# A graph network on one core: ring slots of eight gathered tiles with one store each, and landed slots counted one by one for SyncE

## The reference

```
def spline_conv(x, row, col, basis, idx, W, b):
    z = jnp.einsum('ni,kio->nko', x, W).reshape(N * K, Fout)        # K = 125
    gathered = z[col[:, None] * K + idx]
    msg = jnp.einsum('es,eso->eo', basis, gathered)
    out = jax.ops.segment_sum(msg, row, num_segments=N)
    deg = jax.ops.segment_sum(jnp.ones_like(msg[:, 0]), row, num_segments=N)
    return out / jnp.maximum(deg, 1.0)[:, None] + b

h = elu(spline_conv(ones, row, col, basis, idx, stn1_w, stn1_b))
h = elu(spline_conv(h, row, col, basis, idx, stn2_w, stn2_b))       # phase c2 below
t = elu(h @ stn3_w + stn3_b) @ stn4_w + stn4_b
new_pseudo = clip(pseudo + t[col] - t[row], 0, 1)
x = x + spline_conv(x0, row, col, basis2, idx2, conv_w, conv_b)     # phase c3 below
x = x + gat_and_gru(layer_norm(x), src, dst, ...)
```

## Time and profile before

| | us |
|---|---|
| median of 3 runs | 15551.18 (15526.23 to 15558.94) |
| the profiled execution's own time | 15572.58 |
| its span, first to last instruction | 15570.9 |
| phase c2, first gather to last store / to the last `c_mix_sb` | 5283.4 to 7840.8 / 7929.9 |
| phase c3, first gather to last store / to the last `c_mix_sb` | 8207.0 to 11303.6 / 11367.5 |
| PE, DVE, ACT, POOL busy over the whole span | 54%, 46%, 16%, 57% |

### The profile page before, as it was taken

One profiled execution on the slowest core, in us unless ns is written; L12 is line 12 of the kernel. 1 busy time (PEld: TensorE's weight loads), 2 busy tenths in 40 slices (PEclk: granted clock), 3 DMA queues, 4 the chain that ended last, 5 costly groups with the idle time before them and its releaser, 6 DMA issues. The chain is left out here.

```text
span 15570.9 us, 217238 instructions
## 1 busy us (share of the span) xinstructions
PE 8388.0 (54%) x58520; PEld 7268.8 (47%) x58520; DVE 7182.0 (46%) x16568; ACT 2542.0 (16%) x7161; POOL 8827.4 (57%) x7652
## 2 busy tenths in 40 slices
PE   1346666666466589898863555554520000009996
PEld 1335555555366477777743444444420000009994
DVE  5984444444388666665533455454420000035553
ACT  0002222222100133333321222221200000000001
POOL 0015555555344588888817888888837777732220
PEclk9996666666688799999966667676755555557775
DMA  0000000000511244444413233333311111111110
GB/s 19 0 1 2 2 2 2 2 2 2 8 28 28 60 92 92 93 93 93 91 24 47 45 48 48 47 48 48 48 24 27 27 27 27 26 41 33 33 33 8
DMA packets 1795083, 554.18 MB, mean 36 GB/s; under 512 B 1620582, under 2 KB 1736774, under 8 KB 1794403
## 3 DMA queue, kind: packets, MB, share of 16 engines
q1 hardware_dynamic: 1071972, 306.93, 10.7%
q0 software_dynamic: 241536, 196.63, 7.2%
q10 hardware_dynamic: 481536, 50.16, 3.0%
HBM read 398.94 MB, written 153.86 MB: 36 GB/s over the span
## 5 line engine op out<-in xcount | busy, mean ns | idle before, releaser
L1063 PE MATMUL c_acc<-c_spread_sb,c_basis_sb 128*125 128x256 f32 (+1 forms) x12544 | 2608.7, 381 | 1221.3 <-DVE c_basis_sb L979 1007.2
L1063 PEld LDWEIGHTS c_acc<-c_spread_sb,c_basis_sb 128*125 128x125 f32 x12544 | 2328.6, 238 | 1470.1 <-issue 1277.0
L864 POOL DMA_INDIRECT c_ring<-feat_table,c_at x1568 | 2288.6, 1460 | 464.7 <-issue 463.6
L491 POOL DMA_INDIRECT rec<-rk_rec,rk_place x1568 | 1598.0, 1019 | 1463.8 <-ACT rk_rec L466 1023.7
L558 POOL DMA_INDIRECT g_ring<-gat_table,g_record x1568 | 1623.9, 1036 | 751.9 <-issue 544.8
L864 POOL DMA_INDIRECT c_ring<-hid_table,c_at x1568 | 1745.7, 1113 | 464.7 <-issue 462.2
L1102 ACT ACTIVATE c_sums<-c_acc 125x512 f32<-125x512 f32 (+1 forms) x3136 | 1497.9, 491 | 2381.3 <-PE c_acc L1063 1913.6
L436 PE MATMUL rk_look_ps<-rk_table,rk_lo_t 128*128 128x98 f32 x3136 | 1051.4, 434 | 1116.4 <-ACT rk_table L470 695.4
L964 DVE TENSOR_TENSOR c_spread_sb<-c_mark,c_rin 128x512 f32<-128x512 f32 (+1 forms) x3136 | 1619.1, 550 | 0.0
L436 PEld LDWEIGHTS rk_look_ps<-rk_table,rk_lo_t 128*128 128x128 f32 x3136 | 726.6, 288 | 1485.4 <-DVE rk_before L398 1062.7
L1075 PE MATMUL c_mix<-c_sums,c_w 125*64 125x128 f32 (+1 forms) x18816 | 1135.6, 281 | 401.2 <-issue 293.6
(11 more groups left out here) (320 smaller groups left out, 14079.8 us busy)
## 6 DMA issues: line engine op xcount, KB each, us to landing
c_rin<-rows SPq DMA_DIRECT2D x3136, 42.0 KB
c_rin<-rows SPq DMA_DIRECT2D x3136, 20.0 KB
rows<-c_ring POOLq DMA_DIRECT2D x392, 128.0 KB
at_rin<-rows SPq DMA_DIRECT2D x98, 360.0 KB
rows<-c_ring POOLq DMA_DIRECT2D x392, 72.0 KB
rows<-g_ring ACTq DMA_DIRECT2D x196, 144.0 KB
rec<-rk_rec,rk_place POOLq DMA_INDIRECT x1568
c_ring<-hid_table,c_at POOLq DMA_INDIRECT x1568
```

The costliest lines, as they stand in the source:

```text
L491: pool.indirect_dma_start(out=d.rec, out_offset=bass.IndirectOffsetOnAxis(ap=place[:, u, j:j + 1], axis=0), in_=rec[:, u, j, :], in_offset ...
L864: pool.indirect_dma_start(out=ring[:, u, j, :], out_offset=None, in_=table, in_offset=bass.IndirectOffsetOnAxis(ap=at[:, h, u, j:j + 1], a ...
L1063: last = pe.matmul(acc[pp % BANKS][:, (w % 2) * WN * feats:(w % 2 + 1) * WN * feats], basis[:, q, w, :, :].rearrange("p a b -> p (a b)"), ...
```

## The change

`SLOT` goes from 4 to 8. The ring keeps four slots, so it is twice as large, a turn is 32 tiles, and there are 49 turns. A slot's rows are stored by one transfer of 8 x 128 rows. The gathers are the same 1568 in each phase.

POOL no longer waits for a slot's store just before it fills that slot again. After each store it waits for the store of the slot before that one (`slot_done`), and adds one to a new semaphore `done`. `c.need` now counts slots of 8 tiles instead of turns of 16, and SP waits once, for `done`, in place of its four waits. The loop over passes on POOL is gone (the gathers are made once for all passes; with this data there is one pass before and after).

```
-SLOT = 4
+SLOT = 8
 TILES = RING * SLOT
 TURNS = NT // TILES
-TURN_BITS = (TILES * P).bit_length() - 1
+SLOTS = NT // SLOT
+SLOT_BITS = (SLOT * P).bit_length() - 1
...
-                    chain(dve.tensor_scalar(need[:, :], block_fill[:, 1:NB + 1], float(P + TILES * P - 1), float(EP),
+                    chain(dve.tensor_scalar(need[:, :], block_fill[:, 1:NB + 1], float(P + SLOT * P - 1), float(EP),
...
-            def store_slot(o, t, u):
-                pool.wait_ge(gathered[u], (o * TURNS + t) * (16 * SLOT) + 16 * SLOT)
+            def store_slot(t, u):
+                pool.wait_ge(gathered[u], t * (16 * SLOT) + 16 * SLOT)
                 pool.sem_inc(pool_turn, 1)
                 pool.dma_start(rows_v[:, bass.ds(t * TILES + u * SLOT, SLOT), :], ring[:, u, :, :]).then_inc(stored[u], 16)
 
-            def later_turn(o, t, h):
-                pool.wait_ge(at_made, o * TURNS + t + 1)
-                for u in range(RING):
-                    pool.wait_ge(stored[u], (o * TURNS + t) * 16)
-                    pool.sem_inc(pool_turn, 1)
-                    if u == RING - 1 and not (isinstance(t, int) and t == TURNS - 1):
-                        take_places(t + 1, 1 - h)
-                    gather_slot(h, u)
-                    if u:
-                        store_slot(o, t, u - 1)
-                    else:
-                        store_slot(o, t - 1, RING - 1)
...
+            def slot_done(t, u):
+                pool.wait_ge(stored[u], t * 16 + 16)
+                pool.sem_inc(done, 1)
+
+            def turn_of_slots(t, h, first=False, last=False):
+                pool.wait_ge(at_made, t + 1)
                 pool.sem_inc(pool_turn, 1)
                 for u in range(RING):
+                    gather_slot(h, u)
+                    if u == 2 and not last:
+                        take_places(t + 1, 1 - h)
+                    if not (first and u == 0):
+                        store_slot(t if u else t - 1, (u - 1) % RING)
+                    if not (first and u < 2):
+                        slot_done(t if u >= 2 else t - 1, (u - 2) % RING)
+
+            take_places(0, 0)
+            turn_of_slots(0, 0, first=True)
+            with pool.Fori(0, TURNS // 2 - 1) as i:
+                turn_of_slots(i * 2 + 1, 1)
+                turn_of_slots(i * 2 + 2, 0)
+            turn_of_slots(TURNS - 2, 1)
+            turn_of_slots(TURNS - 1, 0, last=True)
+            store_slot(TURNS - 1, RING - 1)
+            slot_done(TURNS - 1, RING - 2)
+            slot_done(TURNS - 1, RING - 1)
...
-                turns = sp.value_load(need[0:1, bass.ds(b, 1)], min_val=1, max_val=TURNS)
-                for u in range(RING):
-                    sp.wait_ge(stored[u], (o * TURNS + turns) * 16)
-                    sp.sem_inc(sp_turn, 1)
+                slots = sp.value_load(need[0:1, bass.ds(b, 1)], min_val=1, max_val=SLOTS)
+                sp.wait_ge(done, slots)
+                sp.sem_inc(sp_turn, 1)
```

More of the change, by code:

```diff
@@ L275, in _ @@
                 if k == 0:
-                    chain(dve.tensor_scalar(need[:, :], block_fill[:, 1:NB + 1], float(P + TILES * P - 1), float(EP),
+                    chain(dve.tensor_scalar(need[:, :], block_fill[:, 1:NB + 1], float(P + SLOT * P - 1), float(EP),
                                             ALU.add, ALU.min))
                     chain(dve.tensor_copy(c.need[:, :], need[:, :]))
-                    chain(dve.tensor_scalar(c.need[:, :], c.need[:, :], TURN_BITS, None, ALU.logical_shift_right))
+                    chain(dve.tensor_scalar(c.need[:, :], c.need[:, :], SLOT_BITS, None, ALU.logical_shift_right))
                 chain(dve.tensor_tensor(block_size[:, :], block_fill[:, 1:NB + 1], block_fill[:, 0:NB], ALU.subtract))
@@ L807, in flow_conv @@
     at_made = sem(f"{name}_at_made")
+    done = sem(f"{name}_done")
     pool_turn = sem(f"{name}_pool_turn")
@@ L887, in _ @@
[L887 to L890, removed]
+            def slot_done(t, u):
[3 more added lines that the diff above has]
+                pool.wait_ge(at_made, t + 1)
                 pool.sem_inc(pool_turn, 1)
                 for u in range(RING):
[L893 to L902, removed]
-                for u in range(RING):
-                    pool.wait_ge(stored[u], o * (TURNS * 16) + TURNS * 16)
-                    pool.sem_inc(pool_turn, 1)
+                    gather_slot(h, u)
[5 more added lines that the diff above has]
+                        slot_done(t if u >= 2 else t - 1, (u - 2) % RING)
@@ L1044, in _ @@
                 offsets.step(dve, o)
-                dve.tensor_scalar(need[:, :], need[:, :], float(TURNS), float(TURNS), ALU.add, ALU.min)\
+                dve.tensor_scalar(need[:, :], need[:, :], float(SLOTS), float(SLOTS), ALU.add, ALU.min)\
                     .then_inc(need_ready, 1)
```

## The result

| | us, median | range | runs |
|---|---|---|---|
| before | 15545.08 | 15526.23 to 15558.94 | 4 |
| after | 17138.68 | 17079.42 to 17161.82 | 4 |

The ratio is 1.102, 95% interval 1.099 to 1.1051. The forecast was 15408 us. The experiments ran on five chips, and they fall into two kinds, told by the kernel before: three take 15514 to 15783 us for it (kind I, as here), two take 14767 to 14866 (kind II). On kind II the changed kernel took 14533 us in its one run, beside 14866 for the kernel before (11 runs, none under 14856), 2.2% less.

The account below looks back on a forecast made before the run. The prediction took POOL to bound c3, and PE to have almost no room in a nearly balanced c2. Gains of 118 us (c3) and 25 (c2), 143 together, took the median 15551 to 15408 us; range 15320 to 15510.

Parts of the forecast that it names:

- As long as it runs I keep the blocks' pace (26.4): c2: blocks stay 26.4 us apart while POOL runs; POOL ends 128 us sooner, so 4.8 more blocks run at 23.1: 16 us.
- 25 us of gain: c2's whole gain: 16 us for blocks at the faster pace, plus 12 for earlier data, less 3 of lag.
- the 12 us for data that come earlier: c2: some of DVE's 391 us of load waits fall away, from 0 to 98 us, taken as 12.
- The terms of c3: c3: 121 us from fewer stores plus 7 from fewer copies, less 10 of lost shadow, a gain of 118 us.
- forecast 121: c3: 392 stores become 196 with a bar of 1.00 us, so POOL's 317.3 us of stores fall by 121.
- forecast 7: c3: 49 copies of places instead of 98 save between 0 and 13 us, taken as 7.
- stores in the shadow of DVE: c3: stores next in line when DVE starts are free; with fewer stores 32 us free become 22, a loss of 10.
- The store's bar: POOL's time for one store, both phases: 0.81 us for 512 rows, extrapolated to 1.00 for 1024.
- Rival 3: POOL is held inside the larger store; at a bar of 3.0 us, 16020 us in all; chance 0.09.
- whose rule I weighed: Stores on POOL: many descriptors before incremental cost shows, so the bar stays near 0.81; gain 188 us, time 15363.
- The moved waits: POOL's wait for a store, now after the next slot's store, costs nothing, hidden by eight gathers.
- Rival 1: The store's bar is flat, or c2's PE follows POOL: gain 188 to 274 us, about 15350 us; chance 0.25.

Follow-up runs that it names:

- e14: Slots of four tiles in the second convolution (c2), eight in the third (c3), done count in both; kind II: 14734 us against 14866 before, ratio 0.9909.
- e15: The changed kernel, unedited, run again as a control on a chip of kind II: 14533 us, beside 14866 for the kernel before.
- e4: The changed kernel with SLOT = 4, keeping its new done count and waits; kind I: 15520 us, beside 15563 for the kernel before.
- e13: The changed kernel with c2's gathers taking 144 bytes a row instead of 256, computation partly left out; kind II: 14539 us, beside 14866 before.
- e18: The changed kernel with c2's gathers replaced by plain loads of 128 table rows, computation partly left out; kind II: 14377 us, beside 14767 before.
- e3: The changed kernel with each slot of eight stored by two transfers, both behind the eight gathers; kind I: 16030 us, beside 15563 before.
- e10: The changed kernel with about 0.7 us of zeroing on POOL after the fourth of each eight gathers in c2; kind I: 15535 us, ratio 1.0009.
- e11: The changed kernel with about 0.37 us of zeroing on POOL after the fourth of each eight gathers in c2; kind I: 15978 us, beside 15514 before.
- e12: The changed kernel with about 0.7 us of zeroing on POOL right behind each store in c2; kind I: 15875 us, beside 15514 before.

## Why the prediction was wrong

**The step that failed** is one sentence on c2: "As long as it runs I keep the blocks' pace (26.4)". I took the pace as PE's own, and POOL as its neighbour that only hands over rows. On kind I the runs show otherwise. After 7340, where DVE hardly waits for loads any more, the blocks are 26.5 us apart while POOL gathers and 23.1 when it has stopped: 23.1 is PE's own pace and 3.4 are hindrance by POOL. The change alters the hindrance: it went to 354 - 23 = 331 us a block. 25 us of gain were forecast for c2, 1662 us of loss were measured.

On kind II there is next to no hindrance (5 us of "issue" waits of PE in e14, 13 in e15), and another step of the same sum failed: the 12 us for data that come earlier, which took c2's blocks as PE's. There the blocks go at POOL's pace, and c2 gained 214 us over slots of four on the same chip (e14 to e15). POOL itself gained 230: 131 in the stores, 10 in the copies, and 90 in the gathers, whose mean fell from 1.122 to 1.065 us, which I had not forecast and which no run explains.

What should have warned me stood in the earlier trace rows: pace 26.3 and 26.5 while POOL runs, 23.1 as soon as it stops, with PE at a clock of 0.97 against 1.00. I used the 23.1 for the last blocks and put the rest to POOL being late now and then. But DVE's waits for loads were gone after 7340 at the same pace, so lateness was no cause of it there. PE had 111 us of "issue" waits in 1800 us of before's c2, which the prediction does not weigh.

**The terms of c3** were right in mechanism and too large in sum. POOL goes from 9868.0 to its last store at 12894.3, 3026 us where there were 3097: 70 less, where I had 118. By the earlier trace rows: stores 317.3 - 185.0 = 132 (forecast 121, since the bar was 0.944 and not 1.00); copies 26.0 - 11.8 = 14 (forecast 7); the gathers 64 longer (2352.5 against 2288.6; forecast 10 for "stores in the shadow of DVE"); the gaps ahead of gathers 14 longer, since each went from 0.297 to 0.305 us. 132 + 14 - 64 - 14 = 68. The mis-sized term is the shadow; why a gather is 40 ns longer in the mean, while its median stays 955, was not tried.

**The store's bar.** 0.668, 0.81 and 0.944 us for 128, 512 and 1024 pieces. Rival 3 (POOL held inside a large store) did not come: none of 392 is over 0.972. The Trainium skill, DMA: Bandwidth & Descriptors, section "Anatomy of one DMA", whose rule I weighed, would have it near 0.81; the trace lies between that and my line, nearer to mine.

**The moved waits** cost nothing, as forecast. The profile puts 36 gaps in c2 and 24 in c3 down to a store (11.0 and 7.3 us), but each is 0.31 us long at most, as the gap ahead of any gather is; e4 shows that the new scheme as a whole costs nothing with small slots.

**The rivals.** None of the four was the loss. The slower one had POOL held up; in the runs POOL was faster than before, and the others were held up. Rival 1 (PE follows POOL) is what kind II shows, and beyond its size: up to 274 us by the prediction, 333 measured.

## What to carry to other kernels

When an engine's pace changes at the moment at which another one stops, though it does not wait for that one's data, treat the difference as interference and price a change by what it does to it. GpSimd's indirect gathers in a dense row can hold up every other engine, on some chips (here from 26.4 to 354 us a block): break them into short runs (here four, with a store between) where PE has no room, and lengthen them only where the phase leaves it room. Profile such a change on more than one chip before the sign is believed: the same pair of kernels gave 1.102 and 0.978.

## What the runs showed of the hardware

**Two kinds of chip.** They differ already in an earlier stage whose code is the same, where POOL writes every tile by an indirect transfer, a scatter (L491 before, L492 after). 500 us of it, the kernel before on kind I and the changed kernel on kind II:

```profile
1500.00:2000.00 500.00, 313.77 (x1539) 252.99 (x1539) 207.80 (x1127) 110.49 (x449) 262.22 (x258) 0.61 0.02 2
```

```profile
1500.00:2000.00 500.00, 351.83 (x1892) 288.15 (x1891) 254.83 (x1381) 136.54 (x557) 319.56 (x315) 0.67 0.02 3
```

258 POOL instructions against 315, PE 1539 against 1892, while one such transfer takes 1.02 us on both. c2 begins at 5284 against 4722, which is most of what sets the kernel before apart on the two kinds. With the same kernel, the changed one, on kind I and then on kind II, this stage and c1, where POOL computes and issues no transfers:

```profile
L492 POOL DMA_INDIRECT rec<-rk_rec,rk_place x1568: 956/962/1723, 1075.1 to 4116.6; - x196
...
L492 POOL DMA_INDIRECT rec<-rk_rec,rk_place x1568: 952/958/1724, 1075.3 to 3556.5; - x196
...
L729 POOL TENSOR_TENSOR c_basis_sb<-c_plane,c_keep x196: 2382/2398/2616, 4141.0 to 5223.0; 128x1250 f32<-128x1250 f32 x196
...
L729 POOL TENSOR_TENSOR c_basis_sb<-c_plane,c_keep x196: 2382/2411/2619, 3580.8 to 4661.3; 128x1250 f32<-128x1250 f32 x196
```

3042 us against 2481 with the scatters; 1082 against 1081 without. The attention's gathers take 2168 against 1968. The stages without indirect transfers by POOL agree: the count 790 us on both, the attention sum 1216, the update 257, and a block of c2 after POOL has stopped 23.1 (kind II: e13, e15 and e18). **Among the stages the kinds differ clearly only where POOL issues indirect transfers**, so it seems that a scatter holds the others up as a gather does; no run changed the scatters. c3 has gathers and does not differ in this way, 3088 against 3123.

**How the others are held up.** On kind I, while POOL gathers, SP's instructions, its register work too, often start in steps of about 0.7 us: of 8043 SP instructions in 5500 to 7300 of before, 541 come 0.65 to 0.8 us behind the last; of 9868 in 4900 to 7000 of the changed kernel on kind II, 6. In the hole of the changed kernel, 5500 to 7300, SP has 493 instructions, and 296 of them start 0.65 to 0.75 us after the end of the one before. On PE only the "issue" waits show, no such step. c3 isn't starved on either kind; there DVE's runs stretch gathers to 6.9 us, which breaks POOL's row too. That this is what protects c3 is only argued.

**What stays open.** What in an indirect transfer delays the other engines' instructions, whether plain loads from POOL would do the same on kind I, and what differs between the chips. A backlog that grows in a run of gathers and drains in a break would fit e3, e10, e11 and e12; no row shows it.
